# Four fused graph layers on one core: GpSimd takes over every second group's copy of edge counts

## The reference

```python
edge_index = jnp.stack([src, dst])
h = jnp.maximum(_layernorm(x, axis=-1), 0.0)
x = x + _L0_gnn_ref(h, edge_index, node_vec1, ...)     # 4 blocks of sparse attention and MLP
...
x = x + _L1_gnn_ref(h, L1_gnn_wc, L1_gnn_wn, L1_gnn_bias, edge_index)   # mean over edges
...
x = x + _L2_gnn_ref(h, edge_index, edge_type_2, ...)   # relational, two layers
...
x = x + _L3_gnn_ref(h, L3_gnn_label, edge_index, batch0, ...)           # two layers
```

## Time and profile before

| what | us |
|---|---|
| median of 3 runs (lowest to highest) | 3040.24 (3038.99 to 3043.73) |
| the profiled execution | 3037.72 |
| its span in the trace | 3036.0 |
| PE busy in the span | 2839.1 (94%) |
| DVE busy | 2028.1 (67%) |
| ACT busy | 917.6 (30%) |
| POOL busy | 615.7 (20%) |
| stretch of the group loop | 196 to 364, of which PE 165.75, DVE 162.12, ACT 142.33, POOL 0.00 busy |

### The profile page before, as it was taken

How to read it: one execution, slowest core, us unless ns; L and a number is a source line. 1 busy time by engine, 2 the same in 40 slices (tenths; PEclk the granted TensorE clock), 3 DMA queues, 4 the chain that set the end, 5 groups by cost and what they waited for, 6 DMA issues and landing times.

```text
span 3036.0 us, 31287 instructions
## 1 busy us (share of the span) xinstructions
PE 2839.1 (94%) x11232; PEld 1806.2 (59%) x11232; DVE 2028.1 (67%) x3758; ACT 917.6 (30%) x1315; POOL 615.7 (20%) x494
## 2 busy tenths in 40 slices
PE   2889989998999999999999999999899999999999
PEld 0346656675556676556666555667545566456555
DVE  8889867786746777757776765778787876623211
ACT  4558732223312223212222221222322213213221
POOL 0000043342113334023334031334310000000000
PEclk9899999999999999999999999999999999999999
DMA  4000020002300000400000320000245244420001
GB/s 108 1 1 1 21 77 1 28 1 66 104 21 1 1 28 15 132 32 14 1 28 15 93 70 14 1 28 1 83 118 152 70 134 137 132 78 37 14 1 34
DMA packets 74966, 143.63 MB, mean 47 GB/s; under 512 B 11684, under 2 KB 12107, under 8 KB 74812
## 3 DMA queue, kind: packets, MB, share of 16 engines
q1 hardware_dynamic: 69276, 129.61, 14.3%
q0 software_dynamic: 5536, 12.03, 1.2%
HBM read 130.68 MB, written 10.92 MB: 47 GB/s over the span
## 4 chain that ended last, share of the span: by engine, by line
PE 73%; DVE 17%; issue 5%; ACT 3%; DMA 1%; DVEq 1%; POOL 0%; POOLq 0%; ACTq 0%
PE ps L1680 14%; PE ps L1903 11%; PE ps L1932 10%; PE ps L1774 6%; PE ps L1877 5%; PE ps L1585 5%; PE ps L1652 4%; DVE prob L1087 4%; DVE x L1077 3%; PE ps L1602 2%; PE ps L1924 2%; PE ps L1763 2%; DVE ps L1030 2%; PE ps L1748 2%; ACT prob L1454 2%
## 5 line engine op out<-in xcount | busy, mean ns | idle before, releaser
L721 POOL TENSOR_TENSOR pacc<-pacc,prob 125x628 f32<-125x628 f32 (+1 forms) x288 | 404.8, 1405 | 349.8 <-DVE prob L1106 349.8
L1680 PE MATMUL ps<-yT,w 128*128 128x416 f32 (+1 forms) x1152 | 439.8, 539 | 15.0 <-DVE qk_lo L1021 5.9
L1774 PE MATMUL ps<-prob,big 125*128 125x314 f32 x1280 | 393.7, 430 | 14.1 <-DVE prob L1106 10.8
L1454 ACT ACTIVATE prob<-prob 125x628 f32<-125x628 f32 x320 | 233.0, 728 | 575.1 <-DVE prob L1087 575.1
L1932 PE MATMUL ps<-pieces,counts_r 125*125 125x512 f32 x1400 | 354.5, 407 | 0.0
L1680 PEld LDWEIGHTS ps<-yT,w 128*128 128x128 f32 x1152 | 227.8, 200 | 201.3 <-issue 187.6
L1106 DVE SCALAR_TENSOR_TENSOR prob<-prob,typed 125x628 f32<-125x628 f32 x320 | 260.2, 813 | 70.2 <-ACT prob L1454 67.6
L1932 PEld LDWEIGHTS ps<-pieces,counts_r 125*125 125x125 f32 x1400 | 258.2, 186 | 77.2 <-issue 17.4
L1763 PE MATMUL ps<-qk_hi 128*125 128x314 f32 x640 | 271.4, 424 | 11.5 <-DVE prob L1087 11.3
L1774 PEld LDWEIGHTS ps<-prob,big 125*128 125x128 f32 x1280 | 227.5, 189 | 81.1 <-DVE prob L1106 27.2
L1030 DVE CUSTOM_DVE_ANT_0 ps<-ps,typed 125x628 f32<-125x628 f32 x320 | 257.8, 816 | 8.0 <-PE ps L1748 7.5
(11 more groups left out here) (222 smaller groups left out, 4282.6 us busy)
## 6 DMA issues: line engine op xcount, KB each, us to landing
basis<-in_basis SPq DMA_DIRECT2D x160, 256.0 KB, 2.7
lite_ring<-in_basis SPq DMA_DIRECT2D x120, 256.0 KB, 2.6
w<-in_m_w SPq DMA_DIRECT2D x8, 1024.0 KB, 6.8
w<-in_wk SPq DMA_DIRECT2D x5, 1024.0 KB, 6.3
w<-in_wv SPq DMA_DIRECT2D x4, 1024.0 KB, 5.6
oT<-in_cw SPq DMA_DIRECT2D x8, 512.0 KB, 3.9
w<-in_wq SPq DMA_DIRECT2D x4, 1024.0 KB, 5.6
w<-in_wo SPq DMA_DIRECT2D x4, 1024.0 KB, 5.5
```

The costliest lines, as they stand in the source:

```text
L721: nc.gpsimd.tensor_tensor(pacc[:, c0:c0 + nn], pacc[:, c0:c0 + nn], prob[:, n % 3, p0:p0 + nn], ALU.add).then_inc(psum_done, 1)
L1454: A.activation(prob[:, n % 3, :], prob[:, n % 3, :], ACT.Exp, scale=DH ** -0.5).then_inc(exp_done, 1)
L1680: last = mm(lin_ps(job, 128, nn), weight[:, k, m * 128:(m + 1) * 128], lhs[:, k, c0:c0 + nn], start=(k == 0), stop=(k == KD - 1))
L1774: last = mm(o_halves[:, b, :], vrow[:, t, h * DH:(h + 1) * DH], prob[:, n % 3, b * QUARTER:(b + 1) * QUARTER], start=(t == 0), stop=(t == ...
```

## The change

Groups with an even number keep both copies on ACT. For a group with an odd number, ACT makes the `run` copy alone, and POOL then copies `run[g % RUNS]`, in SBUF and float16 already, to the bucket's place in `typed`. The order of the placements is kept by the one counter `bucket_placed`: POOL's copy of group g waits until it has reached g, and so does ACT's placement of an even group. ACT may write a `run` buffer again only when the group that used it four groups earlier is placed. PE's wait is unchanged.

```diff
@@ gpsimd, after the ten tile_power @@
+            pool.wait_ge(places_ready, 1)
+            for g in range(1, GROUPS, 2):
+                place = pool.value_load(placei[0:1, g:g + 1], min_val=0, max_val=PLACE + (T - 1) * N)
+                pool.wait_ge(run_ready, g + 1)
+                pool.wait_ge(bucket_placed, g)
+                nc.gpsimd.tensor_copy(typed[:].bitcast(F16)[:, bass.ds(place, N)], run[0:P, g % RUNS, :]).then_inc(bucket_placed, 1)
@@ scalar @@
             for g in range(GROUPS):
                 if g == 0:
                     act.wait_ge(places_ready, 1)
-                place = act.value_load(placei[0:1, g:g + 1], min_val=0, max_val=PLACE + (T - 1) * N)
+                mine = g % 2 == 0
+                if mine:
+                    place = act.value_load(placei[0:1, g:g + 1], min_val=0, max_val=PLACE + (T - 1) * N)
                 act.wait_ge(*((group_full, g) if g else (onehot_used, STEPS)))
+                if g >= RUNS:
+                    act.wait_ge(bucket_placed, g - RUNS + 1)
                 A.activation(run[0:P, g % RUNS, :], ps[0:P, (g % 2) * 1536:(g % 2) * 1536 + N], ACT.Copy).then_inc(run_ready, 1)
-                if g:
-                    A.drain()
-                A.activation(typed[:].bitcast(F16)[:, bass.ds(place, N)], ps[0:P, (g % 2) * 1536:(g % 2) * 1536 + N],
-                             ACT.Copy).then_inc(bucket_placed, 1)
+                if mine:
+                    if g:
+                        act.wait_ge(bucket_placed, g)
+                    A.activation(typed[:].bitcast(F16)[:, bass.ds(place, N)], ps[0:P, (g % 2) * 1536:(g % 2) * 1536 + N],
+                                 ACT.Copy).then_inc(bucket_placed, 1)
```

## The result

The changed kernel takes 3055.58 us (median of 5 runs, 3055.38 to 3060.92) against 3040.24 before (5 runs, 3038.74 to 3046.32). The ratio is 1.005, with a 95% interval of 1.0039 to 1.0062: slower by half a per cent, some 15 us. The forecast was 3066, with a range of 3047 to 3098. The profiled execution took 3055.4 us, its span is 3053.7, 17.7 more than before.

A forecast was written before the change was run, and what follows sets the result against it. A PE-ACT ring bounds the loop at 5.54 us per pair; with the change DVE does, at 5.34 work plus 1.10 standing, 6.44. Times 29 that adds 26.1 to 3037.72, plus 2.5 to the median: 3066 us, range 3047 to 3098.

The forecast's parts named there:

- A ring of PE and ACT's second copy: Group loop: PE and ACT wait on each other, setting a pair of groups at 5.54 us.
- The prize of 5.8 us: Group loop: relieving ACT of 29 typed copies gains at best 0.20 us per pair, 5.8 us.
- The copy: POOL's copy of 125 x 1250 float16 in the loop: 1.24 us taken, 0.72 and 2.27 kept for the range.
- DVE stands while POOL copies: Group loop: POOL's copy holds DVE's SBUF instructions, as POOL additions behind the loop did, for 1.10 us per pair.
- DVE's floor: Group loop: DVE's work per pair taken as twice 2.67, or 5.34 us.
- the sum: Group loop: 5.34 us of DVE work plus 1.10 standing, 6.44 per pair against 5.54; 26.1 us in all.
- D: Rival, group loop: POOL's copies are cheap (0.72 us) but still hold DVE; 5.92 per pair, 3051 us; chance 0.08.
- C: Rival, group loop: a one-input POOL copy doesn't hold DVE; 3039 us, or 3034 if quicker than 1.07; chance 0.10.
- point of decision: Group loop: the change is faster only if a copy costs DVE under 0.20 us (5.54 less 5.34).
- B: Rival, group loop: POOL's copy takes 2.27 us and holds DVE 2.13; pair 7.47, about 3096 us; chance 0.14.
- starvation: Group loop: POOL is not starved by back-to-back DVE work; its small operations got their turn after 0.17 to 0.24 us.
- up to 0.6 us: Group loop: longest time POOL's copy waits for the DVE instruction in hand, within a chain of 5.5 to 6.1 us.

The follow-up runs named there:

- e4: Kernel before, both copies on ACT, but placement reads the run buffer in SBUF and PE waits only for the run copy: 3034.67 us, ratio 0.9976.
- e2: Changed kernel with POOL's copies left out and all waits kept, POOL only counting bucket_placed up: 3034.28 us, ratio 0.9978.
- e1: Kernel before plus 29 POOL copies of odd groups' run buffer into a dead buffer, awaited only by that run buffer's reuse: 3054.8 us, ratio 1.0044.
- e5_half: Changed kernel with POOL copying only the first 625 of 1250 columns of an odd group: 3044.76 us, ratio 1.0027.
- e5_words: Changed kernel with POOL copying the same bytes as 625 int32 words instead of 1250 float16 numbers: 3046.51 us, ratio 1.0023.
- e6: Changed kernel with POOL placing all 59 groups and ACT making only the run copies: 3082.85 us, ratio 1.0137.
- e3: Changed kernel where PE rewrites an odd group's PSUM region after ACT's run copy, without waiting for POOL's copy: 3055.52 us, ratio 1.005.

## Why the prediction was right, and by how much it was off

**What bounds the kernel now: right.** A ring of PE and ACT's second copy at 5.54 us, a floor for PE at 5.34: e4 and e2 take exactly the wait out and land at 5.34 per pair and 3034 us. The prize of 5.8 us was about 7. Only PE's floor is 5.34, though; DVE's is lower, as is shown below.

**The copy: right.** 1.24 us was taken from the iota and the selects; 1.228 was measured. The additions with two inputs would have given 2.27. By the traces it costs 1.23 us for 1250 numbers and 0.74 for 625, so 0.79 ns more per number. The estimate from the Trainium skill's page GPSIMD Engine Reference, section 3.1 (about 1.8 cycles per element, 1.88 us), is not what this copy does; nearer is that section's other rate, 1.03 cycles for the simplest bodies, an estimate of 0.86 ns per number.

**DVE stands while POOL copies: right, and it is the cause.** It was read off two additions behind the loop. What was open, whether a copy with one input does the same, is shown by e1. The Trainium skill's page SBUF — State Buffer, section on the two separate sides, says so, and the trace agrees: 0.25 us of work took 1.23. The standing was 0.99 us where 1.10 was estimated. `carry` asks 0.04 us after the copy's start, and its 0.25 us of work end at 304.21, so they began 0.21 us ahead of the copy's recorded end, where the earlier trace rows gave 0.14.

**DVE's floor: the term that was mis-sized.** This is the larger of the two errors in the sum, 0.20 us of 0.31. It took 5.34 us of DVE work per pair, twice the 2.67 between two `onehot_dst` in the earlier trace rows, because DVE showed no gap there. It is 5.14. The tiles one by one, before:

```profile
304.41 0.55 DVE L995 TENSOR_SCALAR onehot_src<-col_iota,es 128x1250 f16<-128x1250 f16 x1
304.94 0.55 DVE L995 TENSOR_SCALAR onehot_src<-col_iota,es 128x1250 f16<-128x1250 f16 x1
305.48 0.55 DVE L995 TENSOR_SCALAR onehot_src<-col_iota,es 128x1250 f16<-128x1250 f16 x1
```

And after:

```profile
306.70 0.54 DVE L1002 TENSOR_SCALAR onehot_src<-col_iota,es 128x1250 f16<-128x1250 f16 x1
307.16 0.54 DVE L1002 TENSOR_SCALAR onehot_src<-col_iota,es 128x1250 f16<-128x1250 f16 x1
307.61 0.54 DVE L1002 TENSOR_SCALAR onehot_src<-col_iota,es 128x1250 f16<-128x1250 f16 x1
```

An instruction of 0.54 us can start 0.46 us after the one ahead of it; they overlap by 0.08. Before, they started 0.53 and 0.54 apart, and so did PE's steps. PE's matmuls in the kernel before, each row beginning with the last matmul of a step, the one that gives a tile of the ring back:

```profile
304.11 0.48 PE L1652 MATMUL ps<-onehot_src,onehot_dst 128*125 128x226 f16 x2
304.65 0.48 PE L1652 MATMUL ps<-onehot_src,onehot_dst 128*125 128x226 f16 x2
305.18 0.48 PE L1652 MATMUL ps<-onehot_src,onehot_dst 128*125 128x226 f16 x2
```

These are the steps four tiles back, and DVE's three tiles above start 0.30 us after them: at each, DVE was waiting for PE to give back a tile. In the whole loop 172 of the 232 tiles behind the first four start so, 0.04 us after the recorded end of that matmul. (The ring was not enlarged to try it.) A wait of 0.08 us eats only the overlap, so no idle time shows. In the other half of the pair (the four tiles from 307.23) the first two start 0.46 apart before the change too. After the change no tile of the steady loop follows PE in this way. So a whole group is 2.57 us (305.95 to 308.52) and not 2.67. With 5.14 and 0.99 a pair is 6.13; 6.14 was measured. That is 0.60 more than 5.54, and 29 times that is 17.4 us. The loop as a whole grew by 15.3 only, mainly because its first eight groups, slow already before, grew by 0.9 us (24.0 to 24.9) where four pairs would have made 2.4. That 17.4 on the profiled 3037.72 comes so near to the 3055.4 of the profiled execution is chance: 2.4 us of the difference between those two executions lie outside the loop.

**How far off.** The loss was forecast at 26.1 us and came as 15.3. Of the 10.8 between them some 9 are the pair (6.44 against 6.13), the rest mostly the loop's first groups. The time is in the range, but the low end of the range was put there for D, a cheap copy that is not the case here, and not for an error in DVE's floor.

**The rivals.** C, that a copy leaves DVE alone, is out by e1; its point of decision, 0.20 us of standing, should read 0.40 with the true floor (5.54 less 5.14). e5_half stands at 0.47 and its pair is 0.07 longer, just beyond. B (2.27 us) is out by the copy's length. D's cheap copy exists, but only when asked for in int32 words: e5_words took 0.74 us where 0.72 was estimated for it. That no starvation comes in is right for the change: POOL's copies are recorded with 1.228 us at the median and 1.329 at most. But "up to 0.6 us" for POOL's wait was too low as a bound. With twice the copies (e6) POOL waits 0.95 us, and at the start of e3's loop once for longer:

```profile
204.16 1.91 DVE L1002 TENSOR_SCALAR onehot_src<-col_iota,es 128x1250 f16<-128x1250 f16 x4
204.43 3.32 POOL L671 COPY typed<-run 125x1250 f16 x1 [51.80 <-ACT run L1396]
205.98 0.68 DVE L992 TENSOR_TENSOR onehot_dst<-col_iota,es 128x500 f16<-128x500 f16 x1
206.56 1.23 DVE L997 TENSOR_SCALAR carry<-ident,same 125x125 f16<-125x125 f16 x1
```

The copy is recorded from 204.43 to 207.75. If its work took 1.23 us as elsewhere, it had waited some 2.1 us, through four `onehot_src` tiles and nearly all of `onehot_dst`.

**What the profile should show.** The loop was to grow by 26 us and grew by 15.3 (165.5 to 180.8). The held instruction was expected to be an `onehot_src`; it is `carry` in 27 of the 29 pairs (its 58 instances are busy for 41.2 us where 58 times 0.25 is 14.5; the surplus is 27 times 0.99). One `onehot_src` is held, for 1.51 us in all, near the expected 1.6. ACT's wait for PE is 2.6 us per pair, as said. PE's wait for POOL was to be less than its wait for DVE's tiles; the table has it the other way round (25.1 against 20.6), and only e3 shows that it costs nothing.

## What to carry to other kernels

In this loop work moved to GpSimd was not free for VectorE: 1.23 us of copy cost it 0.99. Where VectorE issues float16 SBUF instructions back to back, price a GpSimd copy as if VectorE did it, and ask whether VectorE has that slack in the pair, not in the span. Before taking an engine's spacing for its floor, compare it with the shortest spacing of equal instructions anywhere in the trace: the first tiles of a group started 0.46 us apart already in the kernel before. No idle time in the profile doesn't mean no waiting. And if a second copy holds up the reuse of PSUM, let it read the first copy in SBUF: it took a few lines and gained what the offloading was after.

## What the runs showed that was not expected

- GpSimd's copy went by the number of elements and not by bytes: 625 float16 took 0.735 us, 625 int32 words 0.742, and 1250 float16 numbers, the same bytes as the words, 1.228.
- A GpSimd instruction that only writes (iota, 1.18 us) also holds a VectorE float16 instruction, for 0.74 us of it per pair.
- ACT copies 1250 float16 out of SBUF in 1.25 us, nearly as fast as 1250 float32 out of PSUM (1.21).
- GpSimd's copy can wait for VectorE for longer than one instruction: once some 2.1 us (e3).
- One wait can hide another: 25.1 us of PE waiting for POOL in the table were worth nothing (e3).
